# A longer, earlier engine loop in the projection steps of a spiking attention and expert layer

## What is computed

```python
Q = lif(layer_norm(query @ Wq.T + bq, gq, betaq), 1.0)   # the same for K and V; lif: 0 or 1
qk = einsum('bhld,bhmd->bhlm', Q, K)
attn = Dh - (q_sum + k_sum.T - 2.0 * qk) + log_pe_bias(N, N)
out = lif(einsum('bhlm,bhmd->bhld', attn * scale, V), 0.5)
out = lif(layer_norm(out @ Wo.T + bo, go, betao), 1.0)
...
scores, expert_idx = top_k(softmax(xt @ router_w.T), 2)  # 8 experts
h = einsum('nh,ehd->end', xt, up_proj)
out_e = einsum('end,edh->enh', silu(h[..., :D]) * h[..., D:], down_proj)
```

## Time and profile before

| what | value |
|---|---|
| median of 3 runs | 511.02 us |
| span of the profiled execution, first to last instruction | 510.6 us |
| PE busy | 384.5 us (75%), 2517 matmuls |
| DVE, ACT, POOL busy | 273.3, 232.6, 211.0 us |
| mean granted clock of TensorE | 0.883 |

### The profile page before, as it was taken

One profiled execution on the slowest core, in us unless ns is written; L12 is line 12 of the kernel. 1 busy time (PEld: TensorE's weight loads), 2 busy tenths in 40 slices (PEclk: granted clock), 3 DMA queues, 4 the chain that ended last, 5 costly groups with the idle time before them and its releaser, 6 DMA issues.

```text
span 510.6 us, 9171 instructions
## 1 busy us (share of the span) xinstructions
PE 384.5 (75%) x2517; PEld 312.9 (61%) x2526; DVE 273.3 (54%) x774; ACT 232.6 (46%) x752; POOL 211.0 (41%) x213
## 2 busy tenths in 40 slices
PE   5498773110113999998999999999999999999960
PEld 2234662100112999997778888888888887667650
DVE  5799971000100687996545444554455442458995
ACT  1567421000001788986545544454445543366650
POOL 5242467777771000000233333333333333259993
PEclk9799985555555799999999999999999999999995
DMA  8721223222220111320443344343443332495222
GB/s 269 247 96 41 83 83 125 104 104 104 104 105 31 42 41 41 106 83 1 144 131 121 121 119 136 118 124 113 124 134 123 118 98 74 184 369 193 100 84 83
DMA packets 40432, 58.98 MB, mean 116 GB/s; under 512 B 6294, under 2 KB 27926, under 8 KB 40408
## 3 DMA queue, kind: packets, MB, share of 16 engines
q1 hardware_dynamic: 31712, 38.53, 24.5%
q0 software_dynamic: 6848, 18.70, 10.1%
q10 hardware_dynamic: 1848, 1.47, 0.9%
HBM read 35.79 MB, written 22.89 MB: 115 GB/s over the span
## 4 chain that ended last, share of the span: by engine, by line
PE 54%; issue 21%; DVE 10%; POOL 7%; DMA 3%; ACT 2%; SPq 1%; POOLq 0%; DVEq 0%; ACTq 0%
PE bank L1108 15%; PE bank L1109 14%; PE bank L1110 14%; POOL xres L718 3%; PE bank L1186 3%; PE bank L1251 3%; POOL xres L711 3%; PE bank L1235 3%; DMA xn<-x 2%; DVE xn L787 2%; DVE xst L765 2%; POOL rstd L703 1%; DVE w_f L808 1%; PE bank L1174 1%; PE bank L1195 1%
## 5 line engine op out<-in xcount | busy, mean ns | idle before, releaser
L692 POOL DMA_INDIRECT slot_y<-ey,dest x71 | 68.5, 965 | 214.6 <-ACT ey L554 186.2
L500 ACT ACTIVATE junk<-bank 128x256 bf16<-128x256 f32 x96 | 35.7, 379 | 89.8 <-remote 71.7
L677 POOL DMA_INDIRECT slot_x<-xn,pos x64 | 61.6, 963 | 23.9 <-issue 19.2
L996 DVE TENSOR_TENSOR hid<-gact,bank 128x256 f32<-128x256 f32 x71 | 29.9, 421 | 76.6 <-ACT gact L538 51.0
L1108 PE MATMUL bank<-ew,exT_h 128*128 x142 | 62.6, 441 | 5.6 <-issue 4.3
L1110 PE MATMUL bank<-w_h,xT_l 128*128 128x256 f32 x192 | 56.9, 296 | 11.3 <-issue 11.2
L795 DVE TENSOR_TENSOR xT_l<-xT,xT_h 128x256 fp32r<-128x256 f32 x28 | 12.9, 460 | 98.1 <-issue 54.1
L1109 PE MATMUL bank<-w_l,xT_h 128*128 128x256 f32 x192 | 56.9, 296 | 11.2 <-issue 11.2
L1108 PE MATMUL bank<-w_h,xT_h 128*128 128x256 f32 x192 | 57.1, 297 | 10.5 <-issue 10.4
L538 ACT ACTIVATE gact<-bank 128x256 f32<-128x256 f32 x71 | 27.4, 386 | 63.8 <-PE bank L1110 63.8
L1110 PE MATMUL bank<-ew,exT_l 128*128 x142 | 55.9, 394 | 0.0
(11 more groups left out here) (193 smaller groups left out, 967.9 us busy)
## 6 DMA issues: line engine op xcount, KB each, us to landing
ex<-slot_x SPq DMA_DIRECT2D x71, 129.0 KB
y_tok<-slot_y SPq DMA_DIRECT2D x8, 1024.0 KB, 13.6
ew_f<-experts SPq DMA_DIRECT2D x24, 256.0 KB, 2.6
xres<-x SPq DMA_DIRECT2D x16, 256.0 KB, 2.8
out<-xres SPq DMA_DIRECT2D x16, 256.0 KB, 2.1
xn<-x SPq DMA_DIRECT2D x6, 512.0 KB, 11.7
slot_y<-ey,dest POOLq DMA_INDIRECT x71, 2.8
xn<-x SPq DMA_DIRECT2D x4, 256.0 KB, 3.8
```

The source lines that it names most:

```text
L500: nc.scalar.activation(junk[:, i, :], proj_ps[r][i], ACT.Square, accum_out=ssq[:, r, i:i + 1]).then_inc(s["ssq_done"], 1)
L677: pool.indirect_dma_start(slot_x, bass.IndirectOffsetOnAxis(ap=pos[:, k, t:t + 1], axis=0), xn[:, t, :], None).then_inc(s["scattered"], 16)
L692: pool.indirect_dma_start(slot_y, bass.IndirectOffsetOnAxis(ap=dest[:, m % 4:m % 4 + 1], axis=0), ey[:, m % 4, :], None).then_inc(y_out[m ...
L996: v.tensor_tensor(hid[:, m % 2, :], gact[:, m % 2, :], h_ps[m % 2][:, F:2 * F], ALU.mult).then_inc(s["hid_done"], 1)
```

## The change

The loop of the projection steps starts at step 4 and covers 20 steps (`PEEL, LOOP = 4, 20`) in place of 12 steps from step 8; steps 24 to 31 are written out. POOL splits 10 pieces in place of 8, ACT's early pieces 4 to 9 are spread over steps 0 to 3, and DVE has ten left in the loop and four after it. The rest of the routing moves on DVE from behind step 4 to ahead of the first deviations. All 7 padding scatters go out at t = 1. ACT waits for `bias_set` at step 3 and for `pads_done` at step 7, 11, ... of the loop; PE opens `kv_ps` at step 3. POOL adds 1 to `qT_set` and 4 to `kv_done` at its start, and all waits on the two are raised by as much.

```diff
-POOL_PIECES, PIECE_STEP = 8, 5
-LOOP = 12
+POOL_PIECES = 10
+PEEL, LOOP = 4, 20
+EARLY_PIECES = ((4, 5), (6,), (7, 8), (9,))
+KV_AHEAD = 4
-PAD_TILE = 3
+PAD_TILE = 1
...
+        def in_one_block(eng):
+
+            eng.addr_align(256 if eng is nc.tensor else 128, 0, 0)
+
...
-            for t in range(8):
+            for t in range(PEEL):
                 body(t, t, None)
+            in_one_block(eng)
             with eng.Fori(0, LOOP // 4) as i:
                 for u in range(4):
-                    body(i * 4 + (8 + u), 8 + u, i)
+                    body(i * 4 + (PEEL + u), PEEL + u, i)
...
-            for t in range(8 + LOOP, NT):
+            for t in range(PEEL + LOOP, NT):
...
-            if m < 8 + LOOP and m % 2 == 0:
-                return None
-            n = POOL_PIECES + (m - PIECE_STEP) // 2 if m < 8 + LOOP else POOL_PIECES + (8 + LOOP - PIECE_STEP) // 2 + m - 8 - LOOP + 1
-            return (n + (0 if i is None else i * 2), n) if m >= PIECE_STEP and n < PIECES else None
+            if i is None:
+                n = POOL_PIECES + LOOP // 2 + m - PEEL - LOOP
+                return (n, n) if m >= PEEL + LOOP and n < PIECES else None
+            n = POOL_PIECES + (m - PEEL) // 2
+            return (n + i * 2, n) if m % 2 == 1 else None
...
-            sp.wait_ge(s["kv_done"], NT)
+            sp.wait_ge(s["kv_done"], NT + KV_AHEAD)
...
-                if m == 11:
+                if m == PEEL - 1:
                     act.wait_ge(s["bias_set"], 1)
+                if m == PEEL + 3:
                     act.wait_ge(s["pads_done"], 16 * PC)
...
-                    for n in ((4, 5), (), (6, 7), ())[t]:
+                    for n in EARLY_PIECES[t]:
                         piece_upper(n, n)
...
+            in_one_block(act)
             with act.Fori(2, QUADS) as i:
...
+            pool.sem_inc(s["qT_set"], 1)
+            pool.sem_inc(s["kv_done"], KV_AHEAD)
...
-                if t >= PAD_TILE:
-                    for c in range(2 * (t - PAD_TILE), min(2 * (t - PAD_TILE) + 2, PC)):
+                if t == PAD_TILE:
+                    for c in range(PC):
...
-                if not early(t + half if num(t) else t, 4):
-                    dve.wait_ge(s["kv_done"], t + (half - 3))
+                if not early(t, 2):
+                    dve.wait_ge(s["kv_done"], t + (half - 3 + KV_AHEAD))
...
+            rest_of_routing()
             dve.wait_ge(s["w_parted"], KC)
...
-                if m == 4:
-                    rest_of_routing()
...
-                    dve.wait_ge(s["kv_done"], NT)
+                    dve.wait_ge(s["kv_done"], NT + KV_AHEAD)
...
+            in_one_block(dve)
             with dve.Fori(1, QUADS) as i:
...
-                if not early(t, 1):
-                    pe.wait_ge(s["qT_set"], t)
+                pe.wait_ge(s["qT_set"], t + 1)
...
-                if m == 4:
+                if m == PEEL - 1:
                     open_kv()
...
-                    pe.wait_ge(s["qT_set"], NT)
+                    pe.wait_ge(s["qT_set"], NT + 1)
...
+            in_one_block(pe)
             with pe.Fori(1, QUADS) as i:
```

## The result

| | before | after |
|---|---|---|
| time, median (range) | 511.23 us (509.71 to 511.58) | 518.29 us (517.66 to 519.8) |
| ratio | | 1.0139 (95% interval 1.0109 to 1.0169) |
| span, profiled execution | 510.6 us | 518.0 us (its time: 519.8) |
| granted clock of PE, mean | | 0.87 |

The change makes the kernel 1.4% slower. The forecast was 461 us, with a range up to 517.

What follows compares the result with a forecast made beforehand. The prediction took PE's crawl in written-out steps 5 to 7 under POOL's scatter, between 74 and 165 us, as the bound. Looping from step 4 saves 18.3 steps of 2.70 us: 510.6 - 49.4 = 461 us (chance 0.34), range 432 to 517.

Steps and rivals of the forecast that it cites:

- The loop from step 4: Projection steps 4 to 23: PE keeps its pace in the loop under the scatter, 20 steps of 2.70 us, 54 us.
- the crawl: PE in written-out steps 5 to 7 under the scatter: a matmul every 2.8 us from 73.35, every 0.7 after 161.76, until 165.27.
- gain of 49.4 us: Projections: 5.7 steps left at 165.3 us where the kernel before had 24, so 18.3 steps less at 2.70 us.
- the loop helps nothing: Rival, projection steps: the scatter itself slows PE, step 7's end stays at 165.3 or up to 2.8 later; 512 us, chance 0.28.
- The scatter's start must not slip: POOL ahead of 65.46 us: two more pieces fit inside its wait for the slots; uncovered, each us would cost one.
- alignment: One added jump at most for each of six loops: 0.2 us each at most, 0 in the sum, upper bound 5 us.
- rest of the routing: DVE ahead of step 4's deviations: 10 instructions, 2.8 us, moving step 4 from 67.9 to 70.7 us.
- 2.5 us for a slower clock: PE idles ahead of step 4 and its clock may fall: half of the loss seen after the crawl, 2.5 us.
- pads: Sends 5 to 11: pads_done at about 80.5 us, ACT asks in step 7 at 81: nothing, 2 us if loads land late.
- pieces: Loop and steps 24 to 27: pieces come every second step in the loop, 20 to 23 behind it, as before.
- three raised semaphores: With two increments on POOL, ahead of its first work: nothing.
- a crawl until the next loop: Rival, steps 24 to 31: they run at 0.7 us a matmul until the experts; 546 us, chance 0.09.

Runs made afterwards that it cites:

- e4: e1 with all of the scatter but its first 4 sends and the 7 pads held back until PE has finished the projections: 514.05 us, ratio 1.0036.
- e8: e6 unchanged, on a third chip, where the kernel before took 511.77 us: 462.35 us, ratio 0.9029.
- e12: e5 with nine sends for every five steps (factor 5 / 3), on the chip of e10 and e11: 454.70 us, ratio 0.8888.
- e3: e1 with POOL splitting 8 pieces and not 10 ahead of the scatter, ACT's early pieces set back too: 512.14 us, ratio 1.0004.
- e1: The kernel after with the alignment taken out ahead of the three expert loops, kept ahead of the projection loops: 513.82 us, ratio 1.0037.
- e10: The kernel after, unchanged, on a fourth chip beside e11: 514.54 us, ratio 1.0061.
- e11: e1 again, on the same chip as e10: 513.65 us, ratio 1.0036.
- e2: e1 with the alignment ahead of the projection loops taken out too, so none at all: 514.96 us, ratio 1.0052.
- e9: The kernel after, unchanged, on the chip of e8: 514.63 us, ratio 1.0062.
- e5: e3 with the scatter paced: behind the first 4 sends and the 7 pads, one send for each finished projection step: 471.75 us, ratio 1.0704.
- e7: The kernel after without the alignment ahead of PE's expert loop alone, on the chip of e5 and e6: 442.22 us, ratio 1.0048.
- e6: e5 with three sends for every two steps (factor 2), 1.8 us apart: 455.19 us, ratio 1.0331.

## Why the prediction was wrong

**The step that failed** is the first: "The loop from step 4 takes the written-out code away from under the scatter. I take it that PE keeps its pace inside the loop, by the moment at which the crawl ends." Steps 4 to 7 stood in the loop, and from step 6 on PE crawled in it, at up to 2.8 us a matmul, as it had in written-out code. e4 shows the cause: the same code beside a silent POOL runs at 2.73 us a step. And e8 and e12 show that it is the scatter's rate: at one send every 1.27 us PE is all but stopped, at 1.6 us (e12, on the mean) and at 1.8 us it keeps its pace. The evidence for the loop was one coincidence, the entry into it at 165.27, 9 us behind the end of the DMA traffic. In the kernel after the crawl ends at about 167.5, again 9 us behind the traffic (158.4), and this time in the midst of the loop. The whole gain of 49.4 us hung on this, and the sum without it is the rival "the loop helps nothing", 512 us. The prediction's reading of the earlier trace rows was coarse too, though nothing hung on it: the matmuls don't come every 2.8 us from 73.35 on. Step 6's first ten start from 80.71 to 82.77 at 0.2 us a matmul, and the pace of 2.8 us is reached at about 100.

**The chance of that rival** was 0.28, under the 0.34 of the forecast, though its case was the better one by the rows: PE's own instruction queue hadn't moved under the crawl, and matmuls that had been started were counted late, which no supply of instructions explains. The argument used against it, that POOL's sends do no harm in the expert stage, was met in the same sentence by their spacing, twice as wide, and this was the right answer.

**"The scatter's start must not slip"** took POOL's two further pieces to be covered by its wait for the slots, and as far as POOL goes they were: pieces done at 64.8, wait until 67.17. What the step left out is that the wait is for DVE, and that DVE is held while POOL works: 1.7 us on the routing, net. It said itself that each us there costs one; e3, whose scatter starts 1.9 us earlier than e1's, is 1.7 us faster. The Trainium skill has this in "SBUF — State Buffer", section "SBUF: two separate sides": a VectorE operation with two SBUF inputs and a GpSimd operation that reads SBUF shut each other out of the ports they share for a whole instruction; for the instruction of line 905, which reads two tiles, the trace agrees (1.39 us beside a piece, 0.42 without).

**The alignment** was put at 0 in the sum with an upper bound of 5 us. On record it took 4.6, nearly the bound, of which PE's second jump itself 3.55; in e10 against e11 0.9, the term at its small end. The zero rested on jumps back of 76 to 238 ns, which are jumps to code that PE had just run; the jump that the alignment adds leads ahead, to code it hasn't. The section "Instruction fetch mechanics" of "Runtime: NRT & Kernel Launch" in the Trainium skill was quoted in the prediction for such a stall at a branch, and here the trace agrees, with 1.19 to 4.21 us. The same alignment ahead of the projection loops shows no cost, by e2, and takes 0.31 us of PE's sequencer while PE has a wait before it.

**The rest of the routing** ahead of the spikes was put at 2.8 us on step 4; it starts 4.5 us later (2.8, and the 1.7 of the slots; in e3 it starts at 70.05, 2.1 us later, with a scatter 0.7 us earlier than before). The 2.5 us for a slower clock were mis-sized: step 4 ran at half clock to 76.4 us and took 4.6 us where it had taken 3.0, so 1.6. Before the experts nothing of either is left, as the crawl took it in: in e3, which has this order but not the later slots, the first tiles are turned 0.3 us from where the kernel before has them. The last of the **pads** was sent by 81.3 us (80.5 forecast), and PE was nowhere near step 7: nothing. The **pieces** of the loop and the three raised semaphores: nothing, by e3's ratio of 1.0004. The rival on the other side, a crawl until the next loop, had no place in the trace.

So the span on record is 510.6 + 2.8 (the scatter 1.7 us later at its start and 2.1 at its end, with what follows) + 4.6 (the jump) = 518.0, and the median of 518.29 lies 1.3 us above the range. That it lies above it and not at its upper edge is in part luck of the occasion: the same kernel took 514.6 and 514.5 us on two other chips (e9, e10).

## What to carry to other kernels

A transfer that one engine generates isn't free for the others because it lies beside them: before giving it a place under other work, compare the pace of that work with and without it (holding it back altogether cost nothing here), and then try its spacing: a third of a us more between sends, on the mean, was worth 57 us where there was a crawl. One event that coincides with the end of a stall is no cause; ask which other event ends there in the same trace, and what the stall would look like if the supply of instructions were short. And an alignment ahead of a loop is a jump, maybe into code not yet loaded: look for its own row in the trace, and put it where the engine waits anyway.

## What the runs showed of the hardware

- **Back-to-back indirect sends of POOL slow PE's matmuls, on some chips.** At 1.27 us from start to start PE's matmuls start up to 2.8 us apart and are counted as done up to 55 us late, on four occasions (that of the result, and three of the four of the experiments); at 1.6 us on the mean and more they run at nearly full pace (2.84 us a step, and 2.75 at 1.8 us). On one chip (e5 to e7) the kernel before, with the same sends, took 440.7 us and not 512, and e7's trace has no crawl. Its 17 executions of the kernel before lie between 439.14 and 442.35 us, the 29 beside e1 to e4 between 509.65 and 513.56. By what path POOL holds PE, and what differs in that chip, stays open: no run here tells, nor whether it is the chip or something beside it on the machine.
- **So the better version depends on the chip.** Paced at 1.8 us the kernel is 9.7% faster than before on a chip with the crawl and 3.3% slower on the one without, where the scatter's end is what the experts wait for. The pacing of e12 (11.1% faster with the crawl) wasn't tried there. In e5 to e8 and e12 the time is the end of the scatter plus 280.3 to 280.9 us. In e12 the scatter ended at 174.3, with its first burst slowed by the crawl, which made 7.1 us in e8 against e6 (181.4 and 174.3); without it I estimate 167.2 + 280.5 = 448 us, still 7 us above the kernel before.
- **The crawl outlasts the traffic by 9 us,** before and after alike (156.3 to 165.3, 158.4 to 167.5); in that time PE starts only 8 matmuls. What holds it then isn't shown.
- **The cost of a jump ahead isn't fixed:** PE is idle for 4.21 us at the one ahead of its expert loop in the profiled execution on record, and for 1.19 and 1.22 us in two others of the same kernel. The jump itself takes 3.55, 0.78 and 0.78 us there, 0.31 to 0.32 ahead of the projection loop, and 0.04 to 0.05 on ACT and DVE.
